# Row maxima, cosine row thresholds and the attention block's release moved from VectorE to GpSimd in a four-layer graph kernel

## The reference, cut to what matters

```python
att = Q @ edge_feat.T * scale * H
att = softmax(att, axis=1)
att_scores = att.mean(axis=0)
comp_mask = softmax(0.5 * structural + 0.5 * att_scores) >= th_comp
xn = x_comp / nrm[:, None]
edge_scores = softmax(xn @ xn.T * H, axis=1)
edge_mask = (edge_scores >= th_edge) & comp_mask[:, None]
H_pruned = H * edge_mask
connectivity = H_pruned.sum(axis=1)
```

## Time and profile before

| what | value |
|---|---|
| median of 3 runs | 1855.68 us (1852.35 to 1858.39) |
| the profiled execution's own time | 1855.87 us |
| its span | 1854.1 us |
| TensorE busy | 1579.2 us, 85% |
| VectorE busy | 1204.2 us, 65% |
| ScalarE busy | 675.8 us, 36% |
| GpSimd busy | 28.6 us, 2% |
| DMA | 585.11 MB, 316 GB/s over the span |

### The profile page before, as it was taken

The page is one execution under the profiler, slowest core; times in us unless marked ns, Lnnn a source line. Parts: engine busy times, 40 slices in busy tenths (PEclk is TensorE's granted clock), DMA queues, the critical chain, the costliest instruction groups (busy, mean ns, idle before and its releaser), DMA issues.

```text
span 1854.1 us, 23223 instructions
## 1 busy us (share of the span) xinstructions
PE 1579.2 (85%) x9738; PEld 640.9 (35%) x9738; DVE 1204.2 (65%) x1659; ACT 675.8 (36%) x493; POOL 28.6 (2%) x96
## 2 busy tenths in 40 slices
PE   6789596699999999777778799999997877797895
PEld 2244242334444333222223344443332222232452
DVE  0000301777622787899998899223887999989897
ACT  0000100233311566577760133013664777810341
POOL 0000000000000000000000000000000000000000
PEclk9999899799999999888889999999998888899998
DMA  9959399489599999255559999999993565589994
GB/s 405 427 242 426 159 383 418 149 291 359 193 408 385 391 375 353 74 213 208 210 188 426 426 420 426 383 423 381 375 367 123 196 221 210 200 336 427 425 426 176
DMA packets 61569, 585.11 MB, mean 316 GB/s; under 512 B 6176, under 2 KB 7328, under 8 KB 21280
## 3 DMA queue, kind: packets, MB, share of 16 engines
q1 hardware_dynamic: 61472, 583.71, 79.0%
HBM read 581.99 MB, written 1.70 MB: 315 GB/s over the span
## 4 chain that ended last, share of the span: by engine, by line
PE 49%; DVE 30%; DMA 16%; issue 3%; ACT 2%; POOL 0%; DVEq 0%; SPq 0%; POOLq 0%; ACTq 0%
PE ps L587 47%; DVE pairs L1276 11%; DVE slot L1415 10%; DMA slot<-adj_t 10%; DMA slot<-adj 6%; PE ps L912 2%; DVE slot L1443 1%; DVE slot L1457 1%; ACT pairs L1050 1%; DVE negmax L1287 0%; DVE arena L1390 0%; DVE hats L1457 0%; ACT hats L1082 0%; DVE cur L1462 0%; DVE cut L1408 0%
## 5 line engine op out<-in xcount | busy, mean ns | idle before, releaser
L1276 DVE CUSTOM_DVE_ANT_1 pairs<-ps,slot 128x832 f32<-128x832 f32 x352 | 345.4, 1020 | 31.5 <-PE ps L587 19.8
L587 PE MATMUL ps<-hats 64*128 64x416 f32 x832 | 230.4, 663 | 90.2 <-DVE max L1276 87.8
L1050 ACT ACTIVATE pairs<-pairs,negmax 128x3327 f32<-128x3327 f32 x88 | 270.1, 3070 | 82.3 <-DVE negmax L1287 82.2
L587 PE MATMUL ps<-slot,cur 128*64 128x512 f32 (+1 forms) x1152 | 213.1, 517 | 27.2 <-DVE slot L1443 19.6
L1065 ACT ACTIVATE arena<-pairs,cut 128x3328 fp8e4<-128x3328 f32 x52 | 159.8, 3072 | 87.2 <-DVE cut L1408 87.2
L1415 DVE SCALAR_TENSOR_TENSOR slot<-pairs,cut,slot 128x3327 f32<-128x3327 f32 x52 | 191.1, 3675 | 0.1
L587 PE MATMUL ps<-slot,stat 128*64 128x512 f32 (+1 forms) x672 | 130.0, 539 | 44.0 <-DMA slot<-adj_t 28.2
L587 PE MATMUL ps<-arena 64*128 64x416 f32 x832 | 163.0, 527 | 0.4 <-DVE max L1276 0.4
L587 PEld LDWEIGHTS ps<-hats 64*128 64x128 f32 x832 | 79.1, 219 | 238.6 <-DVE max L1276 182.7
L1111 DVE COPY pairs<-ps 128x640 f32<-128x640 f32 x3 | 2.5, 824 | 229.8 <-PE ps L587 229.8
L587 PEld LDWEIGHTS ps<-slot,cur 128*64 128x64 f32 x1152 | 77.4, 137 | 159.9 <-issue 123.6
(11 more groups left out here) (179 smaller groups left out, 1498.4 us busy)
## 6 DMA issues: line engine op xcount, KB each, us to landing
slot<-adj SPq DMA_DIRECT2D x173, 1664.0 KB, 9.0
slot<-adj_t SPq DMA_DIRECT2D x70, 1664.0 KB, 15.8
arena<-adj_t SPq DMA_DIRECT2D x28, 1664.0 KB, 22.4
arena<-adj_t SPq DMA_DIRECT2D x52, 832.0 KB, 5.4
pairs<-adj SPq DMA_DIRECT2D x19, 1664.0 KB, 12.8
hats<-adj SPq DMA_DIRECT2D x8, 1664.0 KB, 15.2
hats<-adj_t SPq DMA_DIRECT2D x8, 1664.0 KB, 14.3
pairs<-adj_t SPq DMA_DIRECT2D x8, 1664.0 KB, 13.8
```

Of the source, the lines that this page charges most:

```text
L587: return pe.matmul(o, l, r, start=start, stop=stop, skip_group_check=True)
L1050: act.activation(bufs[b][:, 0:N], bufs[b][:, 0:N], ACT.Exp, bias=negmax[:, b:b + 1], accum_out=rowsum[:, b:b + 1]).then_inc(exp_done, 1)
L1276: dve.tensor_tensor_reduce(out=pieces3(bufs[k % len(bufs)], c), in0=pieces_psum(piece_place(name, k, c)[0]), in1=pieces3(slot_of(name, k), ...
```

## The change

The two helpers of VectorE, `product_max` and `cut_of`, are removed. GpSimd gets `row_max` and `row_cut_of`. The maximum of four columns becomes two steps of one column, which pass through a new tile `half_max` and a new semaphore; the memset of `gates` and the threshold follow on the same engine. VectorE gets a new wait ahead of c0 of block k: that `negmax` of block k-2 has been made, since c0 overwrites that block's columns of `max4`. The thresholds' values stay the same.

```diff
+        half_max = sb("half_max", 2, F32)
...
+            def row_max(name, k):
+                g, bufs = PRODUCTS.index(name), products_of(name)
+
+                pool.wait_ge(piece_read, (g * NB + k) * 4 + 4 + 5)
+                m, b = 4 * (k % 2), k % len(bufs)
+                pool.tensor_scalar(half_max[:, k % 2:k % 2 + 1], max4[:, m:m + 1], max4[:, m + 1:m + 2],
+                                   max4[:, m + 2:m + 3], ALU.max, ALU.max).then_inc(half_max_done, 1)
+                pool.wait_ge(half_max_done, g * NB + k + 1)
+                pool.tensor_scalar(negmax[:, b:b + 1], half_max[:, k % 2:k % 2 + 1], max4[:, m + 3:m + 4], -1.0,
+                                   ALU.max, ALU.mult).then_inc(negmax_ready, 1)
+                if name.startswith("att"):
+
+                    pool.memset(gates[:, k % 2:k % 2 + 1], 0.0).then_inc(block_done, 1)
+
+            def row_cut_of(it, k):
+
+                pool.wait_ge(exp_done, (2 * it + 1) * NB + k + 1)
+                one = slice(k % 2, k % 2 + 1)
+                pool.tensor_scalar(cut[:, one], rowsum[:, one], thresholds(it)[1], small["blocked"][:, k:k + 1],
+                                   ALU.mult, ALU.add).then_inc(row_cut, 1)
...
             for it in range(2):
+                for k in range(NB):
+                    row_max(f"att{it}", k)
                 node_softmax(2 * it)
+                pool.wait_ge(diagonal_ready, 2 * it + 1)
+                for k in range(NB):
+                    row_max(f"cos{it}", k)
+                    row_cut_of(it, k)
                 node_softmax(2 * it + 1)
...
                         dve.wait_ge(product_free, g * NB + k - 2 + 2)
+                    if k >= 2:
+
+                        dve.wait_ge(negmax_ready, g * NB + k - 1)
                 dve.wait_ge(piece_ready, (g * NB + k) * 4 + c + 1)
...
-            def product_max(name, k):
-                g = PRODUCTS.index(name)
-
-                dve.wait_ge(piece_read, (g * NB + k) * 4 + 4 + 5)
-                b = k % len(products_of(name))
-                dve.tensor_reduce(negmax[:, b:b + 1], max4[:, 4 * (k % 2):4 * (k % 2) + 4], axis=X, op=ALU.max,
-                                  negate=True).then_inc(negmax_ready, 1)
-                if name.startswith("att"):
-
-                    dve.memset(gates[:, k % 2:k % 2 + 1], 0.0).then_inc(block_done, 1)
-
             def attention_pass(name, weigh):
                 for k in range(NB):
                     for c in range(4):
                         product_piece(name, k, c)
-                    product_max(name, k)
                     if k:
                         weigh(k - 1)
                 weigh(NB - 1)

-            def cosine_pass(name, cut_of, prune):
+            def cosine_pass(name, prune):
                 for k in range(NB):
-                    product_piece(name, k, 0)
-                    if k:
-                        cut_of(k - 1)
-                    for c in range(1, 4):
+                    for c in range(4):
                         product_piece(name, k, c)
-                    product_max(name, k)
                     if k:
                         prune(k - 1)
-                cut_of(NB - 1)
                 prune(NB - 1)
...
-                def cut_of(k):
-
-                    dve.wait_ge(exp_done, (2 * it + 1) * NB + k + 1)
-                    one = slice(k % 2, k % 2 + 1)
-                    dve.scalar_tensor_tensor(out=cut[:, one], in0=rowsum[:, one], scalar=th_edge,
-                                             in1=S["blocked"][:, k:k + 1], op0=ALU.mult, op1=ALU.add)\
-                        .then_inc(row_cut, 1)
-
```

More of the change, by code:

```diff
@@ L353, in build_program @@
         piece_read = sem("piece_read")
+        half_max_done = sem("half_max_done")
         negmax_ready = sem("negmax_ready")
@@ L1339, in _ @@
             for it in range(2):
-                th_comp, th_edge, th_node = thresholds(it)
+                th_comp, _, th_node = thresholds(it)
                 S = {n: t[:, :] for n, t in small.items()}
@@ L1417, in prune @@
                                              op1=ALU.mult, accum_out=S["conn"][:, k:k + 1]).then_inc(pruned, 1)
-                cosine_pass(f"cos{it}", cut_of, prune)
+                cosine_pass(f"cos{it}", prune)
                 dve.wait_ge(pruned, it * PRUNES + NB)
```

## The result

The changed kernel takes 1861.16 us (median of 18 runs, 1857.64 to 1866.57), the kernel before 1854.49 beside it (18 runs, 1852.35 to 1858.39). The ratio is 1.0037 [1.0029, 1.0044]: slower by 6.7 us. The forecast was 1851.0, and a time within 0.3% of the kernel before was called the likeliest. The measured time lies in the range (1843 to 1863), but more than 0.3% slower, the side that had 0.16. The profiled execution took 1862.19 with a span of 1860.4 us, 6.3 above the span before.

A forecast was written before the change was run, and what follows sets the result against it. The prediction took VectorE to bound the cos turns and TensorE's loop the att turns. Its terms, -9.1 - 4.5 + 7.9 + 1.0 = -4.7 on 1855.87, gave 1851.2, or 1851.0 for the median; range 1843 to 1863.

The forecast's parts named there:

- The cos turn: Cos pass, prune to prune: VectorE's turn falls from 7.97 to 7.78 us, gaining 9.1 over 48 turns.
- rival A: Cos pass: GpSimd's loop becomes the bound, VectorE waiting for each threshold; +9.9 us, 1865.8, at a step of 0.39; chance 0.15.
- 7.26 + 2p: Cos pass: length of GpSimd's loop from prune start to next threshold, forecast 7.74 us, just inside VectorE's turn.
- p: Price of a one-column GpSimd step, not in the trace, taken as 0.24 us from the copy.
- First blocks: Start of each cos pass: block 1 is read while block 0's threshold is made; gain 2.26 us per pass.
- Last blocks: End of each cos pass: last exponentials wait for the prune before, nothing covers this; loss 3.95 us per pass.
- The hold of the first step by the prune: Cos pass: GpSimd's first step sits out VectorE's two-input prune, ending 3.78 us after the prune's start.
- Rival C: Cos pass: the prune doesn't hold GpSimd, last blocks lose 0.62 per pass; -11.4 us, 1844.3; chance 0.13.
- B: Rival with short one-column steps, up to 0.18 us, same mechanism as forecast: -6 to -8, 1848 to 1850; chance 0.15.
- Rival D: Att and cos passes: VectorE's pieces hold GpSimd as well; +21.3 us, 1877; chance 0.09.
- VectorE's new wait: Cos turn: the wait on negmax ahead of c0 costs 0.05 us to handle, lengthening 7.68 to 7.73.
- Att pass: TensorE's loop keeps the turn at 4.62 us; the later maximum costs 0.5 per pass at the last block, 1.0 in all.

The follow-up runs named there:

- e4: The changed kernel with one more one-column GpSimd step, result unused, between the two maximum steps in the cos passes: 1877.27 us, ratio 1.0124 to the kernel before.
- e5: The changed kernel with a prune reading one SBUF input, leaving out the multiplication by the adjacency block (another result): 1844.31 us, ratio 0.9937 to the kernel before.
- e1: The changed kernel with maxima and thresholds of the cos passes back on VectorE, so GpSimd serves the att passes alone: 1858.12 us, ratio 1.0014 to the kernel before.
- e9: The changed kernel with 12 unused matmuls on TensorE ahead of each att pass's last column sums: 1862.00 us, ratio 1.0041 to the kernel before.
- e8: The kernel before with only the cosine threshold moved, to ScalarE right behind the exponentials: 1848.35 us, ratio 0.9958 to the kernel before.
- e2: The changed kernel with maximum and memset of the att passes back on VectorE, so GpSimd serves the cos passes alone: 1859.05 us, ratio 1.0022 to the kernel before.
- e7: The kernel before with only the cosine threshold moved to GpSimd, maxima staying on VectorE: 1852.76 us, ratio 0.9987 to the kernel before.
- e11: The kernel before plus one unused one-column GpSimd step per cos pass, behind the last threshold and ahead of the all-reduce: 1874.30 us, ratio 1.0109.

## Why the prediction was wrong, step by step

- **The cos turn** was the step that failed. The prediction put GpSimd's loop at 7.74, inside a turn of 7.78 that VectorE would set, for a gain of 9.1. Measured: the loop is the turn, 7.90 in the mean, and the gain is (7.97 - 7.90) x 48 = 3.4. The rival A is what happened, "GpSimd's loop becomes the bound": e4 and e5 show it. The sum 7.26 + 2p was short by two small terms. p is 0.26 and 0.30, 0.08 more over both. The step ends 0.16 to 0.25 after the prune's end, not 0.10; with the 0.24 of the turn shown that is 0.14 more. The hand-overs gave back 0.05 (0.03 to ScalarE, where 0.09 was taken, and 0.04 to VectorE for 0.03). Together they make 7.91. The margin of the forecast, 0.04, was smaller than either term. VectorE's own turn was put too long as well: without the hold it is 7.69 (e5, granted clock 0.88 over 762 to 954), so neither the 0.05 of the new wait nor the 0.05 of TensorE's low clock shows there. The point from which A was to cost the whole, p = 0.35, left out this release. What spoke against A, the first step slipping in ahead of the prune, didn't come: the prune starts 0.04 after the threshold's end, GpSimd's next step 0.10 after it.
- **First blocks:** forecast 4.33 from c3 to prune(0), a gain of 2.26; measured 4.64 and 1.95. The three steps cost 0.96 (0.39, 0.30, 0.27) in place of 0.72. Right in kind.
- **Last blocks:** forecast 3.95 lost per pass, measured 4.12. Right, and the largest term.
- **The hold of the first step by the prune:** right. e5 removes it with the prune's two-input form, and the first step falls from 3.8 to 0.37. Rival C is excluded by this, and B by the steps' own 0.26 to 0.39. Rival D is too: beside pieces, which read PSUM and one SBUF tile, the step takes 0.36, and att turns are unchanged. One row isn't explained by two SBUF inputs: the first copy of the earlier trace rows, held for 1.04 beside a one-input instruction, which the prediction named under C.
- **VectorE's new wait** was priced at 0.05: in e5 the turn is 7.69 with it, so at most 0.01 shows.
- **ScalarE's load** was read as 6.4 of each turn; the window of the earlier trace rows gives 149.28 us for 24 turns, 6.2. Nothing hangs on it.
- **Att pass:** forecast 0.5 per pass. The exponentials come 0.66 later at the last block, 1.3 for both. The clock of the last columns was left out: 1.5 more in one of two passes of this execution. The att half alone costs 3.3 (e1), where 1.0 was forecast; filling the idle time didn't bring the median down (e9), and e1's trace has 1.5 of late code exchange in one of two passes. How the 3.3 is made up stays open.
- **Left out altogether:** the code exchange ahead of each all-reduce. "GpSimd has nothing else queued behind these steps but the node softmax, which comes later than they do" counted the order on the queue, but not that the all-reduce starts 5.9 at the earliest behind the last one-column step. 1.1 per cos pass, 2.2.

With these terms: -3.4 - 3.9 + 8.2 + 1.3 + 1.5 + 2.2 = +5.9 against 6.3 between the two spans, where -4.7 had been forecast. The time fell into the range only because the range took in most of rival A; the forecast's own mechanism, a turn set by VectorE, didn't come.

## What to carry to other kernels

Before a small step goes to GpSimd, look at which VectorE instruction runs when it is due: beside the prune with its two SBUF inputs the step lasted as long as the prune did, and the chain behind the step counted from its end; beside the one-input TENSOR_SCALAR of the earlier trace rows a copy was held too, and beside the pieces and e5's prune nothing was. Look also at what GpSimd does next in its queue, as another kind of instruction can cost a code exchange that starts only when the last step is done. Here a step between two instructions of ScalarE, on ScalarE itself (e8), needed neither. And a margin of 0.04 us in a loop sum is no margin when its terms are known to 0.1.

## What the runs showed of the hardware

- The code exchange of GpSimd took 5.9 to 6.3 us at the cos passes' ends (the changed kernel, e2, e4, e7), 9.1 in e11 and 10.9 at e1's att end. In the last two, loads of adjacency blocks ran during it (e1: DMA share 0.61 over 735:742; e11: a load issued at 958.64), in the first the load was issued at 960.53, 3.8 into it. That the DMAs slow it was not varied by itself, and the share alone doesn't order the cases: at the changed kernel's first att end the all-reduce came on time 9.4 after the last memset, with a DMA share of 0.76 over 732:741.5. What makes the exchange long stays open.
- Between GpSimd's one-column steps and their neighbours lie 0.10 (own semaphore), 0.03 to 0.04 (to ScalarE or VectorE) and 0.09 to 0.14 (from ScalarE).
- A first step of the maximum, held by the prune, ends 0.16 to 0.25 after the prune's end (25 turns of the first cos pass); e11's step with one SBUF column ends 0.10 after it. The Trainium skill, "SBUF — State Buffer", section "A bandwidth-pool intuition that's wrong (but worth ruling out)", gives about 0.115 after VectorE's end for a case of its own; for the first step of the maximum the trace shows more, for e11's step about the same.
